# Flags of exact weights made by block turns and maxima on VectorE and read from four partitions, in place of sums by products with ones

## What is computed

```python
x = x + _L0_xattn_ref(_layernorm(x), ctx_1024, ctx_1024, mask_BxS2_ik1)
def _tlin(x, w, s):
    return jnp.einsum('bsi,oi->bso', x, w) * s
h = jax.nn.silu(_tlin(x, w1_w, w1_s)) * _tlin(x, w2_w, w2_s)   # 256 -> 1024
h = jax.nn.gelu(_tlin(h, h1_w, h1_s), approximate=False)       # 1024 -> 1024
h = jax.nn.gelu(_tlin(h, h2_w, h2_s), approximate=False)       # 1024 -> 1024
return _tlin(h, w3_w, w3_s)                                    # 1024 -> 256
```

## Time and profile before

| | |
|---|---|
| Median of 3 runs | 364.61 us (364.49 to 366.68) |
| The profiled execution's own time | 364.78 us |
| Its span in the profile | 363.0 us |
| PE busy with matmuls | 357.4 us (98% of the span) |
| DVE, ACT, POOL busy | 180.8, 147.0, 35.3 us |
| First tile, from the first check to the last | 15.9 to 97.3 us |

### The profile page before, as it was taken

How to read it: one execution, slowest core, us unless ns; L and a number is a source line. 1 busy time by engine, 2 the same in 40 slices (tenths; PEclk the granted TensorE clock), 3 DMA queues, 4 the chain that set the end, 5 groups by cost and what they waited for, 6 DMA issues and landing times.

```text
span 363.0 us, 4724 instructions
## 1 busy us (share of the span) xinstructions
PE 357.4 (98%) x1758; PEld 301.9 (83%) x1758; DVE 180.8 (50%) x405; ACT 147.0 (40%) x247; POOL 35.3 (10%) x59
## 2 busy tenths in 40 slices
PE   8899999999999999999999999999999999999996
PEld 7787888888898888888898888888889888888886
DVE  4859336245556763428445845335626662323233
ACT  4888855752135632621143651620214662212120
POOL 7450121000100230001000050000000000000000
PEclk9999999999999999999999999999999999999999
DMA  7899999983710010110263000020111000000001
GB/s 253 278 380 409 433 338 385 435 334 139 251 55 17 3 29 0 18 27 0 43 193 144 1 29 2 0 38 5 28 32 46 14 1 2 0 0 2 0 0 61
DMA packets 27570, 40.17 MB, mean 111 GB/s; under 512 B 17122, under 2 KB 20068, under 8 KB 27364
## 3 DMA queue, kind: packets, MB, share of 16 engines
q1 hardware_dynamic: 26672, 38.95, 30.8%
q10 hardware_dynamic: 868, 0.80, 0.7%
HBM read 35.80 MB, written 13.64 MB: 136 GB/s over the span
## 4 chain that ended last, share of the span: by engine, by line
PE 97%; DVE 2%; issue 0%; POOL 0%; DVEq 0%; POOLq 0%
PE ring L1099 64%; PE ring L1073 16%; PE ring L1118 8%; PE att L1021 2%; PE att L1045 2%; PE ring L1226 1%; DVE x_attn L798 0%; PE att L1253 0%; DVE stats L746 0%; PE ring L1253 0%; PE ring L1235 0%; POOL rstd L398 0%; PE att L1137 0%; PE att L1272 0%; PE att L1011 0%
## 5 line engine op out<-in xcount | busy, mean ns | idle before, releaser
L1099 PE MATMUL ring<-h_hi,weights 128*128 128x512 f32 x512 | 201.2, 393 | 0.2 <-issue 0.2
L1099 PE MATMUL ring<-h_lo,weights 128*128 128x512 f32 x512 | 199.4, 389 | 0.0
L1099 PEld LDWEIGHTS ring<-h_hi,weights 128*128 128x128 f32 x512 | 96.1, 188 | 20.5 <-DVE act L838 0.4
L1099 PEld LDWEIGHTS ring<-h_lo,weights 128*128 128x128 f32 x512 | 96.1, 188 | 19.8
L565 ACT ACTIVATE act<-ring,scales 128x512 f32<-128x512 f32 x64 | 44.1, 690 | 159.4 <-PE ring L1099 159.4
L857 DVE CAST h_hi<-act 128x512 fp32r<-128x512 f32 x64 | 27.3, 426 | 130.3 <-ACT act L565 126.0
L741 DVE TENSOR_TENSOR h_lo<-act,h_hi 128x512 fp32r<-128x512 f32 x96 | 66.5, 692 | 2.3
L1073 PE MATMUL ring<-xn_hi,weights 128*128 128x512 f32 (+1 forms) x140 | 51.6, 375 | 0.2 <-DVE xn_lo L817 0.2
L1073 PE MATMUL ring<-xn_lo,weights 128*128 128x512 f32 (+1 forms) x140 | 51.1, 371 | 0.0
L551 ACT ACTIVATE gate<-ring,scales 128x512 f32<-128x512 f32 x32 | 22.1, 690 | 32.0 <-PE ring L1073 32.0
L838 DVE SCALAR_TENSOR_TENSOR act<-ring,scales,gate 128x512 f32<-128x512 f32 x32 | 24.0, 749 | 14.1 <-PE ring L1073 12.0
(11 more groups left out here) (135 smaller groups left out, 216.2 us busy)
## 6 DMA issues: line engine op xcount, KB each, us to landing
weights<-weights_staged SPq DMA_DIRECT2D x11, 1024.0 KB, 8.8
x_in<-in_x SPq DMA_DIRECT2D x8, 256.0 KB, 3.0
ctx_cols<-in_ctx_cols SPq DMA_DIRECT2D x8, 256.0 KB, 5.1
ctx_rows<-in_ctx_rows SPq DMA_DIRECT2D x4, 512.0 KB, 6.6
out_dram<-residual SPq DMA_DIRECT2D x16, 128.0 KB, 1.7
turned<-in_x_cols SPq DMA_DIRECT2D x3, 512.0 KB, 7.8
turned<-work SPq DMA_DIRECT2D x32, 32.0 KB, 1.9
mask<-in_mask SPq DMA_DIRECT2D x3, 256.0 KB
```

What stands on the lines that cost most here:

```text
L1099: ins = nc.tensor.matmul(bank[:], w, part[:, k].bitcast(dt), start=(k == 0 and part is h_hi[src]), stop=(k == HC - 1 and part is h_lo[src]))
```

## The change

The products with ones go, and with them `sum_flag`, the matrix `ones` and the semaphore `flag_mm`. DVE makes a flag alone, from `low_sums`: it limits the columns of the flag's pieces to 1 and puts them into the first columns of a cleared tile of 128x32 (`flag_cols`), turns that tile in blocks of 32x32 (`transpose`), and takes the maximum of each row. So each of the four blocks of 32 partitions leaves, on its first partitions, whether a piece has low bits there. These are integers, in one column of `seg_flags` for each flag. PE reads the number from the partitions 0, 32, 64 and 96, adds the four and branches on the sum. DVE takes the flags at the same places of its order as before, and now waits for `low_summed` itself.

```diff
-        seg_flags = sb("seg_flags", [P, len(FLAG_PIECES)])
+        seg_flags = sb("seg_flags", [P, len(FLAG_PIECES)], I32)
+        flag_cols = sb("flag_cols", [P, BLOCK])
+        flag_turned = sb("flag_turned", [P, BLOCK])
...
             def take_flag(flag):
 
-                dve.wait_ge(flag_mm, flag + 1)
-                nc.vector.tensor_reduce(seg_flags[0:1, flag:flag + 1], flag_bank(flag)[0:1], axis=AXIS.X, op=ALU.add
+                first, end = FLAG_PIECES[flag]
+                dve.wait_ge(low_summed, end)
+                dve.wait_ge(flag_cleared, 1)
+                nc.vector.tensor_scalar(flag_cols[:, 0:end - first], low_sums[:, first:end], 1.0, None, ALU.min
+                                        ).then_inc(flag_limited, 1)
+                dve.wait_ge(flag_limited, flag + 1)
+                nc.vector.transpose(flag_turned[:], flag_cols[:]).then_inc(flag_blocked, 1)
+                dve.wait_ge(flag_blocked, flag + 1)
+                nc.vector.tensor_reduce(seg_flags[:, flag:flag + 1], flag_turned[:], axis=AXIS.X, op=ALU.max
                                         ).then_inc(flag_ready, 1)
...
+            nc.vector.memset(flag_cols[:], 0.0).then_inc(flag_cleared, 1)
...
                 pe.wait_ge(flag_ready, flag + 1)
-                value = pe.value_load(seg_flags[0:1, flag:flag + 1].bitcast(I32), min_val=0, max_val=2**31 - 1)
-                with pe.If(value == 0):
+                values = [pe.value_load(seg_flags[p:p + 1, flag:flag + 1], min_val=0, max_val=1)
+                          for p in range(0, P, BLOCK)]
+                total = pe.snap(values[0] + values[1] + values[2] + values[3])
+                with pe.If(total == 0):
                     products(F32R)
                 with pe.Else():
                     products(F32)
-
-            def sum_flag(flag):
-
-                first, end = FLAG_PIECES[flag]
-                pe.wait_ge(low_summed, end)
-                nc.tensor.matmul(flag_bank(flag), ones[:], low_sums[:, first:end], start=True, stop=True
-                                 ).then_inc(flag_mm, 1)
```

More of the change, by code:

```diff
@@ L96, in xattn_ffn @@
         low_sums = sb("low_sums", [P, PIECES])
-        seg_flags = sb("seg_flags", [P, len(FLAG_PIECES)])
+        seg_flags = sb("seg_flags", [P, len(FLAG_PIECES)], I32)
+        flag_cols = sb("flag_cols", [P, BLOCK])
+        flag_turned = sb("flag_turned", [P, BLOCK])
         flag_out = sb("flag_out", [P, 2])
-        ones = sb("ones", [P, P])
         stats = sb("stats", [P, ROWS, 6])
@@ L160, in xattn_ffn @@
         rstd_ready = sem("rstd_ready")
-        ones_made = sem("ones_made")
-        flag_mm = sem("flag_mm")
+        flag_cleared = sem("flag_cleared")
+        flag_limited = sem("flag_limited")
+        flag_blocked = sem("flag_blocked")
         flag_ready = sem("flag_ready")
@@ L220, in xattn_ffn @@
         down_mm = sem("down_mm")
-        def flag_bank(flag):
-            first, end = FLAG_PIECES[flag]
[L225 to L229, removed]
         def probs_cols(r):
@@ L382, in _ @@
             nc.gpsimd.tensor_copy(first_ident, ident[:]).then_inc(first_consts, 1)
-            nc.gpsimd.memset(ones[:], 1.0).then_inc(ones_made, 1)
             def make_mask(t):
@@ L1149, in batches @@
                     gate_and_up(0, (0,), dt, 1)
-                    sum_flag(GATE_UP_B)
                     gate_and_up(0, (1, 2), dt, 1)
@@ L1157, in remaining @@
                     gate_and_up(0, (4, 5, 6), dt)
-                    sum_flag(HID1A)
                     gate_and_up(0, (7,), dt)
@@ L1170, in first_tile @@
                 hid1(HID1A, 0, 1)
-                sum_flag(HID1B)
                 hid1(HID1A, 2)
                 hid1(HID1B, 3)
-                sum_flag(HID1C)
                 hid1(HID1B, 4)
                 hid1(HID1C, 5, 6)
-                sum_flag(HID2A)
                 hid1(HID1C, 7)
@@ L1182, in first_tile @@
                 pe.wait_ge(maxed, ROWS)
-                sum_flag(HID2B)
                 hid2(HID2A, 1)
@@ L1189, in first_tile @@
                 pe.wait_ge(probs_evac[1], 1)
-                sum_flag(HID2C)
                 hid2(HID2B, 4)
@@ L1196, in first_tile @@
                 pe.wait_ge(x_attn_done, 2 * ROWS)
-                sum_flag(LAST)
                 hid2(HID2C, 7)
@@ L1307, in _ @@
             first_turn_xn(0)
-            pe.wait_ge(ones_made, 1)
-            sum_flag(GATE_UP_A)
             first_turn_xn(1)
```

## The result

The changed kernel takes 384.53 us (median of 6 runs, 383.53 to 385.89), the kernel before 365.81 us beside it (6 runs). The ratio is 1.0517, with a 95% interval from 1.0495 to 1.0539: 18.7 us slower. The forecast was 377.3, with a range up to 381.5. That is 7.2 us short of the measured time and 6.0 us short of the measured difference (12.7 against 18.7), since the kernel before took 365.81 here and 364.61 when the forecast was made. The direction, the serial loads and the places of the pauses were right. The clock, which the sum left out, was not.

A forecast was written before the change was run, and what follows sets the result against it. PE's matmuls were taken as the bound (busy 357.4 of 363.0 us). Seven bare checks and four late flags, less 4.3 us, added 12.7 to the profiled 364.8, giving 377.3 after the 0.2 above the median; range 373 to 381.5.

The forecast's parts named there:

- check 1 and the batches: First flag check: its load waits for the flag, 2.65 us later, 0.75 given back in later waits; +1.9 us.
- check 2: Second flag check: needs 3.0 us, has 1.6 of cover, and a cold restart costs 0.1; +1.5 us.
- check 3: Third flag check, bare of cover: longer loads and later flag both count in full; +2.6 us.
- checks 4 and 5: Check 4 hides; check 5, whose flag hangs on chunk 1, needs 3.0 + 0.5 and has 2.0; +1.5 us for both.
- 6 and 7: Check 6 hides narrowly behind the matmuls of chunk 3; check 7 stalls much like check 5; +1.9 us.
- Rival 3: Granted clock falls at a PE pause: a 16-matmul chunk at half pace, 3.7 us, so 381; twice, 385; chance 0.06.
- D: Extra PE sequencer time per check for three more serial loads and the sum: 2.15 us, bounds 1.1 to 2.9.
- F: Extra lateness of a flag from DVE's three dependent instructions, counted at checks 1, 3, 5, 7: 0.5 us, bounds 0.2 to 0.7.
- The formula: Whole-kernel loss from seven bare checks and four late flags: 7 D + 4 F - 4.3, giving +12.7 us.
- rival 1: Within a check the later loads overlap, 1.1 us extra per check: +5.4 us, 370; chance 0.07.
- rival 4: Not slower: extra loads cost almost nothing, the nine products gone gain about 2.3 us, 363 at best; chance 0.03.
- rival 2: Loads cost 0.9 us each, cover runs out and checks 6 and 11 stall too: +19 us, 384; chance 0.04.

The follow-up runs named there:

- kept-busy run: The changed kernel with useless matmuls put ahead of check 1 (24 of 256 columns) and check 3 (10 of 512): 379.99 us, ratio 1.0385.
- reversed order: The changed kernel with the four loads of a check in the order of partitions 96, 64, 32, 0: 385.13 us (one execution).
- two loads and the clock kept up: The changed kernel with loads from partitions 0 and 32 only, and 16 useless matmuls of 256 columns ahead of check 1: 368.99 us, ratio 1.0114.
- two loads: The changed kernel with two loads per check, from partitions 0 and 32, and their sum, half the flags unread: 370.89 us, ratio 1.013.
- early flags: The changed kernel with DVE taking seven flags earlier in its order: 376.86 us, ratio 1.0312.
- switching order: The changed kernel with the loads of a check in the order of partitions 0, 64, 32, 96: 388.40 us (one execution).

## Why the forecast was right in its direction and short in its size

**The bound, the order of the loads and the places held.** Matmuls are what ends last (92% of the chain), the loads are serial, and pauses stand at the seven checks named, while 4, 6, 8, 9, 11, 12 and 14 to 16 hide theirs. Step by step, in us of delay that each adds by the trace, with the forecast in brackets: check 1 and the batches 4.6 (1.9); check 2 1.9 (1.5); check 3 2.2 (2.6); chunk 0 behind it 1.6 (0); checks 4 and 5 1.7 (1.5); 6 and 7 2.5 (1.9); 8 0 (-0.2); 9 and 10 2.2 (2.1); 13 1.8 (1.6); 14 to 16 -0.3 (-0.2). Together 18.2 against 12.7. This execution was 0.3 us ahead of that of before when it came to check 1 (the last pause before it is at 14.24 us in place of 14.52), so the delay itself is some 18.5.

**The step that failed first is the one on the clock.** Rival 3 gave "one pause" 3.7 us and a chance of 0.06, as an alternative to the forecast. In the sum of the forecast it stood at nothing. In truth it came on top of the sum, in two stretches in the profile of the kernel after: 2.1 us in the batches behind check 1 and 1.6 in chunk 0, 3.7 together, which is the difference that the kept-busy run shows in those two places. That this equals the rival's 3.7 for one fall is chance: the rival had a whole chunk at half pace, and the fall in chunk 0 cost less than half of that. I argued that the clock had held through the waits of the first microseconds; but the longest of those was 1.2 us, and the pause that I was forecasting myself at check 1 was near 3. A forecast pause should have been handed on to the clock.

**The second is the size of D.** I priced all four loads by 302 ns, from a kernel in which each load comes from the partition of the load before. Loads that change halves take 0.47, two in each check: 2 x 0.17 = 0.34 more, so D is 2.5 and seven bare checks cost 7 x 0.35 = 2.5 us more. No row of before could show that, but the range covered it: its upper end had D at 2.6, and with D at 2.5 alone the sum is 15.2, 379.8 us, inside the range. What the range lacked was room for the clock on top of it. That it "takes in one fall of the clock" was true only with D at 2.15. The forecast's upper end, 16.7, and the measured clock term, 3.7, make 20.4, so a range that added the two would have held the result.

**The third is F.** The three instructions took 0.16, 0.21 and 0.19 us in the ordinary case, as worked out. At check 1 the flag took 1.34 us (15.44 to 16.78) in place of 0.13, so it was 1.2 us later in place of 0.5, because the first of the three took 0.87 beside POOL. Ahead of check 7 it took 0.57, so that flag was 0.4 later again: the pause there is 2.50 us, and 2.08 in the reversed order, where it took 0.17. The rows, by line, for the other two:

```profile
L820 DVE STREAM_TRANSPOSE flag_turned<-flag_cols x9: 211/211/214, 16.3 to 113.4; 128x32 f32<-128x32 f32 x9
...
L822 DVE TENSOR_REDUCE seg_flags<-flag_turned x9: 185/186/190, 16.6 to 113.7; 128x1 int32<-128x32 f32 x9
```

With 2.5 more for D, 3.7 for the clock and 0.7 and 0.4 more for F at the checks 1 and 7 the sum of 12.7 becomes 20.0, against 18.2 to 18.5 of delay in the trace. About half of the difference is at check 3, where 2.2 us were lost and the sum with D = 2.5 has 2.95. Why, and the rest, is open. The formula itself was tried at another point: with two loads and the clock kept up it gave 3.3, and 3.6 us were measured. That agreement is in part luck. In the trace of that run 2.9 us of delay arise from check 1 up to the first matmul of check 3 (3.65, less the 0.7 by which it was late ahead of check 1), where the formula has 2.0, and 0.7 behind, where it has 1.3.

**The rivals.** Overlapping loads (rival 1) and no loss (rival 4) fell, by the starts of the loads, 0.65 us apart behind a load of 0.30 and 0.8 to 0.9 behind one of 0.47. Cover running out everywhere (rival 2) did not happen: checks 6, 8 and 11 hid. The Trainium skill's page "Runtime: NRT & Kernel Launch" (Instruction fetch mechanics) gives about 200 ns per register, for loads from HBM; the steps of 0.65 and 0.8 to 0.9 us measured here, for loads from SBUF, are three to over four times that, and the measurement decides.

## What to carry to other kernels

Price a load into a register by its whole step on the sequencer, here 0.65 us and not the 0.30 of the load alone, and set it against how far the sequencer is ahead at that place; bring the datum ahead by one block of work (7.7 us here) rather than shorten its making. One number for the sequencer is worth several small operations on an engine that has room, and DVE's room, too, must be read at the place itself. Where a forecast puts pauses of some microseconds on PE, add the stretch at the lower clock behind them as a term of its own.

## What the runs showed of the hardware

- A register load from SBUF by PE's sequencer took 0.30 us if the load before it came from the same half of the partitions (0 and 32, or 64 and 96), and 0.47 us if from the other half, in three orders of the four loads, and 0.30 in all of a pair from 0 and 32; the program's first load took 0.48 to 0.49. The cause is open.
- The granted clock fell to 1.2 GHz behind pauses of 3.69 and 2.31 us, and not behind others of 1.76 to 2.50 us in the same execution; in the other versions it fell behind pauses of 1.80 us (reversed order, check 10), 1.86 and 1.88 (early flags and kept busy, check 10), 2.15 (two loads, check 1) and 2.99 (switching order, check 7). Behind a fall a chunk of 16 matmuls took 5.34 us in place of 3.75.
- A limit of two columns took 0.86 to 0.87 us on DVE while POOL converted a piece in 1.04, in the form with one input and in that with two, against a median of 0.16 over all nine flags. A limit of three columns took 0.57 inside POOL's conversion of the mask and 0.15 to 0.17 before or behind it; four reductions of the same columns took 0.65 together beside the same conversion, and 0.66 without it.
